# Masked heads ahead of context remainders; the second attention and the last feed-forward in one block; the last pair stored by rows

## The reference, cut to what matters

```python
def L0_xattn(q, k, v):            # no softmax: scores times values
    Q, K, V = heads(q @ wq.T + bq), heads(k @ wk.T + bk), heads(v @ wv.T + bv)
    ctx = einsum('bhqk,bhkd->bhqd', einsum('bhqd,bhkd->bhqk', Q, K) / dk, V)
    return ln_g * norm(q + ctx @ wo.T + bo) + ln_b
def L0_ffn(x):                    # each of 8 experts takes its 224 best tokens, gelu between two products
    ...
def L1_xattn(q, kv):              # 16 heads of 16 with a softmax over 375 keys
    ...
def L1_ffn(x):                    # top 2 of 8; all share wi and wo, each has a low-rank term
    for e in range(E):
        gate = (top_i == e).sum(-1) * val_sum
        inter = x @ wi.T + bi + (x @ lora_A[e].T) @ lora_B[e].T
        out += gate * (relu(inter) @ wo.T + bo)
x = x + L0_xattn(ln(x), ctx); x = x + L0_ffn(ln(x)); x = x + L1_xattn(ln(x), ctx); x = x + L1_ffn(ln(x))
```

## Time and profile before

| | |
|---|---|
| median of 3 runs | 792.03 us (791.66 to 792.64) |
| profiled execution | 797.7 us |
| its span | 795.8 us |
| TensorE busy | 724.5 us, 91% |
| VectorE busy | 508.4 us, 64% |
| ScalarE busy | 331.1 us, 42% |
| GpSimd busy | 303.1 us, 38% |

### The profile page before, as it was taken

How to read it: one execution, slowest core, us unless ns; L and a number is a source line. 1 busy time by engine, 2 the same in 40 slices (tenths; PEclk the granted TensorE clock), 3 DMA queues, 4 the chain that set the end, 5 groups by cost and what they waited for, 6 DMA issues and landing times. The chain is left out here.

```text
span 795.8 us, 16691 instructions
## 1 busy us (share of the span) xinstructions
PE 724.5 (91%) x6469; PEld 614.1 (77%) x6469; DVE 508.4 (64%) x1262; ACT 331.1 (42%) x685; POOL 303.1 (38%) x222
## 2 busy tenths in 40 slices
PE   4899999979999999999688999888798887999997
PEld 3678888845688988898576777667677776898997
DVE  4788888878751322303567877676678748667564
ACT  2122222148623221132257777666668541423223
POOL 2233344348721332225235778575677200000000
PEclk9999999989999999999898999999899999999999
DMA  9985000136683644441642996657861000000000
GB/s 298 367 163 49 23 24 24 47 103 204 218 169 90 210 144 129 139 119 24 140 120 45 149 162 115 113 105 121 227 129 26 2 1 13 1 24 1 24 12 24
DMA packets 64475, 81.54 MB, mean 102 GB/s; under 512 B 31891, under 2 KB 54803, under 8 KB 62835
## 3 DMA queue, kind: packets, MB, share of 16 engines
q1 hardware_dynamic: 61170, 72.22, 38.2%
q0 software_dynamic: 2816, 3.67, 2.5%
q10 hardware_dynamic: 416, 4.65, 1.5%
HBM read 60.45 MB, written 19.31 MB: 100 GB/s over the span
## 5 line engine op out<-in xcount | busy, mean ns | idle before, releaser
L1877 DVE TENSOR_REDUCE mx<-psum 112x2 f32<-112x750 f32 x128 | 113.6, 925 | 24.6 <-PE psum L2032 24.0
L1778 ACT ACTIVATE probs<-psum 125x448 f32<-125x448 f32 x192 | 92.8, 543 | 23.1 <-PE psum L2057 21.2
L1697 POOL TENSOR_TENSOR half_sum<-probs 125x896 f32<-125x896 f32 x30 | 62.5, 2085 | 55.5 <-ACT probs L1778 55.5
L572 PE MATMUL psum<-w_parts,c_parts 128*125 128x512 f32 x288 | 73.8, 409 | 10.8 <-DVE w_parts L434 10.4
L2057 PEld LDWEIGHTS psum<-qpk,kpk 128*125 128x125 bf16 x768 | 64.3, 145 | 19.4 <-issue 11.3
L2032 PE MATMUL psum<-kpk,qpk 96*112 96x375 bf16 x256 | 65.7, 350 | 14.3 <-DVE mx L1877 9.9
L2057 PE MATMUL psum<-qpk,kpk 128*125 128x112 bf16 x768 | 70.5, 231 | 4.1 <-issue 2.5
L572 PEld LDWEIGHTS psum<-w_parts,c_parts 128*125 128x125 f32 x288 | 53.7, 190 | 24.7 <-DVE w_parts L434 10.4
L1703 POOL TENSOR_TENSOR tile_sum<-half_sum,probs 125x896 f32<-125x896 f32 x30 | 62.7, 2089 | 7.4 <-issue 4.9
L1170 PE MATMUL psum<-we,hT 128*112 128x256 f32 x256 | 60.0, 395 | 0.0
L1015 ACT ACTIVATE hT<-psum,b 128x224 f32<-128x224 f32 x64 | 25.2, 444 | 76.8 <-PE psum L1155 76.8
(11 more groups left out here) (231 smaller groups left out, 1518.5 us busy)
## 6 DMA issues: line engine op xcount, KB each, us to landing
we<-in_we SPq DMA_DIRECT2D x6, 2048.0 KB, 8.8
kparts_d<-kp SPq DMA_DIRECT2D x16, 562.5 KB, 4.6
kpk<-kparts_d SPq DMA_DIRECT2D x16, 562.5 KB, 5.9
ctx_all<-in_ctxT SPq DMA_DIRECT2D x16, 375.0 KB, 5.6
kpk<-kparts_d SPq DMA_DIRECT2D x16, 375.0 KB, 7.6
we<-in_we ACTq DMA_DIRECT2D x2, 2048.0 KB, 13.8
kpk<-kparts_d SPq DMA_DIRECT2D x16, 187.5 KB, 8.5
qparts_d<-qp SPq DMA_DIRECT2D x16, 168.0 KB, 2.7
```

The source lines that it names most:

```text
L572: ins = pe.matmul(banks[B_KV[t]][0:KT, :], parts_of[:, x, k, t * KT:(t + 1) * KT], w_parts[:, k, w], start=(k == 0 and (x, w) == SPLIT[0]) ...
L1697: pool.tensor_tensor(half_sum[:, m], probs[:, m, 0], probs[:, m, 1], ALU.add)\
L1778: act.activation(probs[:, m, t, g * HU * SQ:(g + 1) * HU * SQ], banks[B_ST[u % 3]][0:KT, 0:HU * SQ], ACT.Exp, scale=SCALE)\
L1877: dve.tensor_reduce(mx[:, n % 2, H + 2 * j:H + 2 * j + 2], psum[0:SQ, first:first + 2, 0:SK], AX.X, ALU.max)\
```

## The change

1. First attention, VectorE: `low(i + 1, 0)` moves from before the masked copy to behind it.
2. The third block is gone: its four programs continue the second block's, with no meeting of the engines between them. The storage of the attention is given up and reused at the same place as before. TensorE gets a wait for the last attention output (`x3_done`) ahead of `team_turn(1)`, whose bank that output shares.
3. `first` is split into `first_rows` (six matmuls) and `first_adapters` (three). In the entry, `marked(1)` moves behind all of team 0's products and `first_rows(1, 0)`, and chunks 0 and 1 of team 1 are done in the entry.
4. The order in the entry: on ScalarE `split_high` of piece 8 goes ahead of `relu(0, 4)` and `team_turned(1)` goes behind `hidden_high(0, 2)`; on VectorE `split_low` of piece 8 goes ahead of `hidden(0, 4)`, that of piece 9 ahead of `chosen(0)`, `hidden_low(0, 3)` ahead of `hidden(0, 5)`, `low_low(1)` between `hidden` of chunks 5 and 6.
5. Last team: the gain times bias is added to both sequences ahead of the last products (`biased_rows`), the products of the first sequence end before most of the second's, and each sequence is finished by one instruction and stored by its own DMA.

```diff
@@ first attention, VectorE @@
-                    if more:
-                        low(i + 1, 0)
                     dve.wait_ge(kvh_ps.sem, kvh_ps.at(i))
...
                     if more:
+                        low(i + 1, 0)
                         low(i + 1, 1)
@@ the split of first @@
+    def first_rows(pe, i, f):
...
+    def first_adapters(pe, i, f):
...
@@ SyncE @@
+        for p in range(PAIRS - 1):
+            sp.wait_ge(x4_done.sem, x4_done.at(p))
+            sp.dma_start(out[:, 2 * p:2 * p + 2], x_all[:, 2 * p:2 * p + 2]).then_inc(x4_out.sem, 16)
+        for s in range(2):
+            b = B - 2 + s
+            sp.wait_ge(x4_done.sem, x4_done.at(PAIRS - 1 + s))
+            sp.dma_start(out[:, b:b + 1], x_all[:, b:b + 1]).then_inc(x4_out.sem, 16)
@@ ScalarE, entry @@
             split_high(act, EARLY)
             hidden_high(0, 0)
             hidden_high(0, 1)
-            team_turned(act, 1)
+            split_high(act, EARLY + 1)
             relu(act, 0, 4)
             hidden_high(0, 2)
-            split_high(act, EARLY + 1)
+            team_turned(act, 1)
             relu(act, 0, 5)
...
@@ VectorE, last team @@
+        def biased_rows():
+            dve.wait_ge(gain_done.sem, gain_done.at(NT - 1))
+            for s in range(2):
+                dve.scalar_tensor_tensor(x_all[:, B - 2 + s], bias_row[:], gain[:, (NT - 1) % 2, s:s + 1],
+                                         x_all[:, B - 2 + s], ALU.mult, ALU.add).then_inc(biased_done.sem, 1)
+        def finish_last():
+            for s in range(2):
+                dve.wait_ge(y_ps.sem, y_ps.at(PAIRS - 1 + s))
+                dve.wait_ge(biased_done.sem, biased_done.at(PAIRS - 1 + s))
+                dve.scalar_tensor_tensor(x_all[:, B - 2 + s], y_of(NT - 1, s), gain[:, (NT - 1) % 2, s:s + 1],
+                                         x_all[:, B - 2 + s], ALU.mult, ALU.add).then_inc(x4_done.sem, 1)
@@ VectorE, entry, as it is after @@
+            hidden_low(0, 0); hidden_low(0, 1)
+            split_low(dve, EARLY); split_low(dve, EARLY + 1)
+            hidden(dve, 0, 4); hidden_low(0, 2); turned_low(dve, 1); hidden_low(0, 3)
+            split_low(dve, EARLY + 2); chosen(dve, 0, 1)
+            hidden(dve, 0, 5); low_low(dve, 1); hidden(dve, 0, 6); hidden_low(0, 4); chosen(dve, 1, 1)
+            hidden(dve, 0, 7); hidden_low(0, 5); hidden_low(0, 6); chosen(dve, 2, 1)
+            hidden_low(0, 7); chosen(dve, 3, 1); lows(dve, 1); team_statistics(dve, 2); finish(0)
@@ TensorE @@
+        def products_of_last(i):
+            product(i, 0, range(4, FC - 1))
+            product(i, 1, range(2))
+            product(i, 0, (FC - 1,)).then_inc(y_ps.sem, 1)
+            product(i, 1, range(2, FC)).then_inc(y_ps.sem, 1)
@@ TensorE, entry @@
             first(pe, 0, 4)
+            pe.wait_ge(x3_done.sem, x3_done.at(B - 1))
             team_turn(pe, 1)
             first(pe, 0, 5)
             second(pe, 0, 4)
             gates(pe, 1)
             first(pe, 0, 6)
             second(pe, 0, 5)
             first(pe, 0, 7)
             second(pe, 0, 6)
             pe.wait_ge(w_low.sem, w_low.at(EARLY + 2))
             product(0, 0, range(4))
             second(pe, 0, 7)
-            products_of(0, False, True)
+            product(0, 0, range(4, FC - 1))
+            product(0, 1, range(FC - 1))
+            product(0, 0, (FC - 1,))
+            product(0, 1, (FC - 1,)).then_inc(y_ps.sem, 1)
+            first_rows(pe, 1, 0)
+            marked(pe, 1)
+            first_rows(pe, 1, 1)
+            first_adapters(pe, 1, 0)
+            first_adapters(pe, 1, 1)
```

More of the change, by code:

```diff
@@ L1580, in marked @@
         ins.then_inc(marks_ps.sem, 1)
-    def first(pe, i, f):
+    def first_rows(pe, i, f):
         c = cols_of(i)
-        dst = banks[f % 4][:, 0:c]
         if f >= 4:
@@ L1588, in first @@
             pe.wait_ge(hs_done.sem, hs_done.at(i, 0))
-        if f == 0:
-            pe.wait_ge(lows_done.sem, lows_done.at(i))
         if i == 0:
@@ new lines, in two_layer_kernel @@
+    keys_ctx.close()
+    ctx = ExitStack()
+    hnT_parts = sb(ctx, "hnT_parts", [128, 2, 2, KC, MOST * SQ], F32R)
+    low_parts = sb(ctx, "low_parts", [E1 * R1, 2, MOST * SQ], F32R)
+    hs_parts = sb(ctx, "hs_parts", [128, 2, FC, MOST * SQ], F32R)
+    low1 = sb(ctx, "low1", [E1 * R1, 2, MOST * SQ], F32R)
+    low21 = sb(ctx, "low21", [E1 * R1, 2, MOST * SQ], F32R)
+    wi_last = sb(ctx, "wi_last", [128, 2, KC, FP], F32R)
+    wo_parts = sb(ctx, "wo_parts", [128, 2, FC, D], F32R)
+    biased = sb(ctx, "biased", [SQ, 2, D])
@@ new lines, in _ @@
+    @block.sync
+    def _(sp):
+        for p in range(PAIRS - 1):
[5 more added lines that the diff above has]
+            sp.dma_start(out[:, b:b + 1], x_all[:, b:b + 1]).then_inc(x4_out.sem, 16)
+        sp.wait_ge(x4_out.sem, x4_out.at(PAIRS))
+    @block.gpsimd
+    def _(pool):
+        for i in range(2, NT):
+            inverse_root(pool, i)
@@ new lines, in _, with hidden_high, body, entry @@
+    @block.scalar
+    def _(act):
+        def hidden_high(i, f):
+            c = cols_of(i)
+            act.wait_ge(hs_done.sem, hs_done.at(i, f + 1))
+            if f == 0 and i:
+                act.wait_ge(y_ps.sem, y_ps.at(first_pair(i) - 1))
+            act.activation(hs_parts[:, 0, f, 0:c], hs[:, f % 4, 0:c], ACT.Copy).then_inc(hs_high.sem, 1)
+        def body(i, more):
+            for f in range(FC):
+                relu(act, i, f)
+                if more and f == 5:
+                    gate_exp(act, i + 1)
+                if f >= 2:
+                    hidden_high(i, f - 2)
+                if more and f == 2:
+                    team_turned(act, i + 1)
+                if more and f == 4:
+                    low_high(act, i + 1)
+            for f in (FC - 2, FC - 1):
+                hidden_high(i, f)
+        def entry():
+            split_high(act, EARLY)
+            hidden_high(0, 0)
+            hidden_high(0, 1)
+            split_high(act, EARLY + 1)
+            relu(act, 0, 4)
+            hidden_high(0, 2)
+            team_turned(act, 1)
+            relu(act, 0, 5)
+            hidden_high(0, 3)
+            split_high(act, EARLY + 2)
+            low_high(act, 1)
+            relu(act, 0, 6)
+            hidden_high(0, 4)
+            gate_exp(act, 1)
+            relu(act, 0, 7)
+            for f in range(5, FC):
+                hidden_high(0, f)
+        entry()
+        for i in range(1, NT):
+            body(i, i + 1 < NT)
```

334 lines of the change are left out of this document (141 added, 193 removed).

## The result

The changed kernel took 784.74 us (median of 20 runs, 777.94 to 797.0), the kernel before 792.28 (20 runs, 787.41 to 803.76); the ratio is 0.990 with an interval of 0.988 to 0.993. That is 7.5 us less, where 8.4 had been forecast. Executions of both kernels scatter by 4 us and more, so a few tenths of a per cent can't be read from times here; the traces can be read to 0.05 us at the places that were edited, and they carry what follows.

The account below looks back on a forecast made before the run. TensorE, busy 91% of the span, was taken as the bound, with gains only in its idle or half-clock time and behind its last matmul. 0.84 + 6.2 + 1.4 = 8.4 us off the 792.03 median gave 783.6 us, range 781.0 to 787.6.

Parts of the forecast that it names:

- Edit 1: First attention, masked copy first: 0.21 us a pair, four of six pairs counted, 0.84 us; ends 0.4 and 1.26.
- So the moved step itself costs nothing: First attention: the moved remainder ends some 0.7 us later, covered by 3.4 us of TensorE work; uncovered, 0.6 a pair.
- the wait for the store of `z`: First attention, pairs 2 and 3: VectorE idles 0.76 us until it lands, so what pairs 1 and 2 gain is lost.
- Edits 2 to 4, the layout: Seam of second and third block: at full clock, team 2's transposes start 7.8 us earlier, at 669.4 us.
- The four gaps: TensorE's remaining waits at the seam: 0.75, 0.9, 1.0 and 0.8 us, where five gaps made 7.5 us.
- Edits 2 to 4, the clock: Seam: one half-clock stretch remains, 1.6 us back from 7.8, leaving 6.2 us; ends 4 and 8.
- rival (a): Seam: no half-clock stretch remains, gain 10.0 us, time 782.0 us; chance 0.22.
- The sign of over 7 us at half clock: Seam: the prediction is wrong if the clock shows over 7 us at half rate there.
- Edit 5: Behind the last matmul: 1.16 us less on VectorE plus 0.25 for the halved transfer, 1.4 us; ends 1.1 and 1.5.
- Rival (b): Seam: VectorE becomes the bound, steps slip 1 us, two half-clock stretches stay; gain 5.8 us, time 786.2; chance 0.25.
- (c): Seam: the blocks' meeting was no loss and the new order does nothing; gain 2.2 us, time 789.8; chance 0.06.
- (d): Seam: the entry stays at half clock from the gates to team 2's transposes; 5 us slower, 797 us; chance 0.04.

Follow-up runs that it names:

- seam_alone: Changed kernel without the masked copy first and without the rows' own stores, so edits 2 to 4 alone: 789.94 us, ratio 0.998 (0.994 to 1.002) to the kernel before.
- before_again: The kernel before, unchanged, traced once more; one run, 793.24 us.
- before: The kernel before the change and its first trace: median 792.28 us of 20 runs; the profiled execution took 797.7 us.
- edits_1_and_5: The kernel before with only the masked copy first and the rows' own stores, three blocks kept: 790.81 us, ratio 1.001 (0.997 to 1.005).
- after_third: The changed kernel, unchanged, traced a third time; one run, 792.41 us.
- pair0_remainder_first: Changed kernel, but in pair 0 the context remainder stands ahead of the masked copy as before: 785.48 us, ratio 0.994 (0.990 to 0.998).
- last_pair_one_store: Changed kernel with the last pair's two rows stored by one DMA of 224 KB behind the second row: one execution, 786.73 us.
- after: The changed kernel and its first trace: median 784.74 us of 20 runs; the profiled execution took 782.44 us.
- after_again: The changed kernel, unchanged, run again for a second trace: 786.6 us (12 runs), ratio 0.992 (0.988 to 0.995).

## Why the prediction was right or wrong

**What bounds the kernel: right.** The gain lies where TensorE had idled or run at half clock, and behind its last matmul; teams 2 to 4 are the same 114.4 to 114.6 us in every trace.

**Edit 1: mis-sized, 0.84 forecast, 0.46 measured between traces without a wait for `z`.** The 0.21 for a pair is right, all six pairs have it: from pair 3's product to pair 7's it is 70.2 us against 70.85. Two steps failed. "So the moved step itself costs nothing" was worked out for pairs with a predecessor's tail; pair 0 has none, and there the remainder had been hidden in a wait of VectorE and now costs 0.85. I had looked for the cover on TensorE's side alone, not for what stands behind the step in VectorE's own order. And the wait for the store of `z` is no constant: in seam_alone and six of the others it is absent, in before_again it is 0.14 and costs TensorE nothing, and in before, edits_1_and_5, after_third, pair0_remainder_first and last_pair_one_store it takes 0.2 to 1.2 from pair 1's product to pair 3's. So 6 x 0.21 - 0.85 = 0.41 in an execution without that wait (measured 127.77 to 127.31), 0.13 between the traces of before and edits_1_and_5, which both have it, and 1.07 between those of before, which has it, and after, which has not. That the forecast of 0.84 lies between is luck.

**Edits 2 to 4, the layout: right.** 25.25 us laid out, 25.35 measured, from durations of before alone. The gain that the prediction took from it, 7.8, counts the transposes of before from the chain's 677.30; by the timeline's 677.13 it is 7.7, and 7.55 to 7.7 was measured. VectorE begins `lows(1)` 18.5 us behind the seam's start, where over 20.5 was the sign of being wrong. The four gaps were forecast as 0.75, 0.9, 1.0 and 0.8 and came out as 0.54, 0.87, 0.89 and 0.43. The first is smaller since ScalarE's chain is 0.1 shorter and TensorE arrives 0.1 later than laid out. The four are 0.7 us shorter together than forecast and TensorE's work as much longer; the distance holds because VectorE's times, which end three of the gaps, were laid out right (12.6 and 20.5 us behind the seam's start, measured 12.63 and 20.61). The move of piece 8 ahead of the two copies does cost a gap in front of the gates, as said.

**Edits 2 to 4, the clock: right on average, not in each execution.** One stretch was taken to remain, at 1.6 us; four traces of six have it, at 1.65, right behind the gates as said, and two have none, which was rival (a). Mean seam 26.5, before 33.0: 6.5, forecast 6.2. The two stretches of before are in all its traces; by TensorE's busy time they cost 2.8 together, where the prediction had 3.3. The sign of over 7 us at half clock did not come in any trace of this order. The rule of the Trainium skill ("TensorE: Matmul & The Clock Gate", section "HAM oscillation") on long pauses would have had none left; the measurement decides, since the stretch came four times though the one gap of the seam ahead of it was 0.54 us and none was over 0.92.

**Edit 5: 1.4 forecast, 1.5 measured.** VectorE's part is 1.1 (0.52 us behind the last matmul against 1.64), forecast 1.16. The transfer is at the upper end of its 0 to 0.37, 0.36 and not 0.25; the 0.25 was a choice within these ends. The estimate of 0.26 goes by a fit of the Trainium skill ("DMA: Bandwidth & Descriptors", section "Anatomy of one DMA") of 2.0 us plus bytes over 436 GB/s. The page gives that fit for DMAs that GpSimd issues, and SyncE issues these; the measurement has 0.36, and the whole landed in 2.2 us.

**The sum.** By the traces 0.46 + 6.5 + 1.5 = 8.5, by the times 7.5 in the first comparison and 7.3 over the 68 and 29 runs; the 1 us between the two is less than the runs can settle. The forecast of 783.6 is 1.1 under the 784.74 measured. That the sum fits the traces to 0.1 is partly luck: edit 1 is 0.4 less, the clock 0.3 and the end 0.1 more. Rival (b) (its terms add up to 5.7, not 5.8) has no support, VectorE is as fast as laid out; (c) and (d) did not happen. The 5.7 us by which the profiled execution lay above the median can be placed: against before_again, 4.5 us shorter, its stretch between is 5.4 us longer and its first attention 0.6. Half-clock time (47.8 us against 37.5) and the pauses without a releaser (8.9 against 7.0) are both longer in it; what makes them vary is open.

## What to carry to other kernels

A new order of three engines can be laid out on paper from the durations of the old trace and comes out within 0.1 us in 25, if every engine's own queue is followed, though single gaps were off by up to 0.4; so cost an edit by the engine whose order it changes, and do it also for the first turn of the loop, where that engine may have been idle. A gain ahead of a transfer that lands at a fixed time is given back there, and the cure is in the queue that issues it. When runs scatter by more than the gain, measure the distance between two landmarks in several traces and keep the total for the sign; and say so where the total, as in seam_alone, does not agree.

## What the runs showed of the hardware

In the new order the granted clock fell to half (1.2 GHz of 2.4) in four traces of six, behind one gap of 0.54 us and the gates' sixteen matmuls with 8 columns, while their four with 448 ran. It stayed there for 3.4 us and cost 1.65 us. The changed kernel itself, the same program each time, shows it in two executions (after_again, after_third) and not in the third (after); in the old order, with 7.5 us of gaps, it came twice in each of three. And a DMA's issue can hold its queue: behind the context loads and three small tables one store's issue took 11.4 to 12.4 us in SyncE's queue, against 0.36 when it went ahead of the tables and the last two loads.
